# Second layer's weighing carried into the next head, and three short groups in the context preparation

## What is computed

```python
# prepared once from the context
K1, V1 = ctx @ Wk1 + bk1, ctx @ Wv1        # second layer, 16 heads of width 16
K3, V3 = ctx @ Wk3 + bk3, ctx @ Wv3        # last layer
V2     = ctx @ Wv2                         # third layer, 16 heads of width 64
# second layer's cross attention, for each head h of 16
s   = q[h] @ K1[h].T / 4 + fside[0, h]     # 128 x 12544, fside is an input of 103 MB
p   = exp(s - max(s));  att[h] = (p @ V1[h]) / sum(p)
# second layer's state space: a causal filter of length 128, the sum of 64 exponentials per channel
```

## Time and profile before

| what | value |
|---|---|
| median of 3 runs | 3325.09 us (3325.0 to 3327.77) |
| profiled execution, its own time | 3318.68 us |
| its span, first to last instruction | 3317.0 us |
| mean granted TensorE clock | 0.965 |
| busy: PE, DVE, ACT, POOL | 92%, 45%, 44%, 7% |
| context preparation | from the start to about 770 us |
| second layer's cross attention | about 1005 to 1517 us |
| third layer's cross attention | about 1600 to 2638 us |

### The profile page before, as it was taken

How to read it: one execution, slowest core, us unless ns; L and a number is a source line. 1 busy time by engine, 2 the same in 40 slices (tenths; PEclk the granted TensorE clock), 3 DMA queues, 4 the chain that set the end, 5 groups by cost and what they waited for, 6 DMA issues and landing times. The chain is left out here.

```text
span 3317.0 us, 66321 instructions
## 1 busy us (share of the span) xinstructions
PE 3054.6 (92%) x23699; PEld 1942.3 (59%) x23699; DVE 1481.3 (45%) x4098; ACT 1471.5 (44%) x2522; POOL 247.3 (7%) x178
## 2 busy tenths in 40 slices
PE   7999999998787999998899999999999887999979
PEld 5555555556484666664455555555555674666678
DVE  2223232321525777765333333333333326888632
ACT  2333333333313888883144444444444432656621
POOL 3231313130000000000000000000000002000000
PEclk9999999999897999999899999999999987999979
DMA  7878787877248999964311111111111254565355
GB/s 227 250 253 255 253 256 254 254 243 228 88 172 327 369 372 359 362 266 166 152 40 41 55 58 39 58 58 39 58 58 39 84 181 116 148 157 147 100 189 193
DMA packets 303301, 577.59 MB, mean 174 GB/s; under 512 B 79666, under 2 KB 249432, under 8 KB 291928
## 3 DMA queue, kind: packets, MB, share of 16 engines
q1 hardware_dynamic: 303204, 576.36, 51.4%
HBM read 395.34 MB, written 180.97 MB: 174 GB/s over the span
## 5 line engine op out<-in xcount | busy, mean ns | idle before, releaser
L1644 DVE TENSOR_SCALAR_CACHE_REDUCE all_S<-l2x_scores 128x448 f32<-128x448 f32 x448 | 261.1, 621 | 413.8 <-PE l2x_scores L1559 413.8
L1708 ACT COPY early_nat_in<-l2x_key_bank 128x448 f32<-128x448 f32 x224 | 119.2, 532 | 486.5 <-PE l2x_key_bank L1546 484.5
L1546 PE MATMUL l2x_key_bank<-ahead_ctx,early_nat_out 128*64 128x448 f32 x1536 | 331.0, 552 | 0.0
L500 PE MATMUL prep_work<-prep_wv,prep_ctxT 128*128 128x512 f32 x688 | 299.9, 594 | 0.0
L887 DVE CUSTOM_DVE_ANT_0 all_S<-l1x_scores,l1x_bias 128x448 f32<-128x448 f32 x448 | 261.9, 621 | 74.4 <-PE l1x_scores L799 67.4
L1138 DVE TENSOR_REDUCE l3x_rowmax<-l3x_scores 128x1 f32<-128x448 f32 x448 | 263.5, 623 | 39.6 <-PE l3x_scores L1058 38.1
L1220 ACT ACTIVATE l3x_pT<-l3x_turned 128x896 f32<-128x896 f32 x224 | 205.0, 918 | 170.3 <-PE l3x_turned L1066 167.1
L1582 PEld LDWEIGHTS l2x_out<-l2x_pT,l2x_v_half 128*64 128x64 f32 x3136 | 203.5, 137 | 96.8 <-issue 96.6
L954 ACT ACTIVATE all_S<-all_S,l1x_negmax 128x896 f32<-128x896 f32 x224 | 232.8, 1042 | 48.5 <-DVE l1x_negmax L900 33.1
L1723 ACT ACTIVATE all_S<-all_S,l2x_negmax 128x896 f32<-128x896 f32 x224 | 233.7, 1044 | 25.2 <-DVE l2x_total L1662 23.8
L1559 PE MATMUL l2x_scores<-early_nat_in,early_nat_out 64*128 64x448 f32 x896 | 229.1, 588 | 8.9 <-ACT early_nat_in L1708 8.2
(11 more groups left out here) (652 smaller groups left out, 4264.6 us busy)
## 6 DMA issues: line engine op xcount, KB each, us to landing
l1x_bias<-in_fside_Bx16xSxS_dram SPq DMA_DIRECT2D x112, 896.0 KB, 6.9
scratch_k<-prep_kparts SPq DMA_DIRECT2D x84, 672.0 KB, 3.3
l1x_k_half<-scratch_k SPq DMA_DIRECT2D x32, 1568.0 KB, 9.7
l2x_v_half<-scratch_v SPq DMA_DIRECT2D x32, 1568.0 KB, 6.3
l3x_k<-scratch_k SPq DMA_DIRECT2D x32, 1176.0 KB, 7.2
scratch_k<-prep_kparts SPq DMA_DIRECT2D x56, 448.0 KB, 4.8
scratch_v<-prep_st_v SPq DMA_DIRECT2D x12, 2048.0 KB, 9.1
scratch_v<-prep_st_v SPq DMA_DIRECT2D x12, 1536.0 KB, 7.2
```

Source lines behind the costliest of these rows:

```text
L500: last = nc.tensor.matmul(w[:, h, :], ctxT[:, k, j * P:(j + 1) * P], wv2[:, k, h * 512:(h + 1) * 512], start=(k == 0), stop=(k == KT - 1))
L1546: last = nc.tensor.matmul(keys_ps[half * VW:(half + 1) * VW, 0:HB], wk_cur[:, k, :], ahead.piece[c // 2][:, k, cols], start=(k == 0), stop ...
L1644: nc.vector.tensor_scalar(com.S[:, b * HB:(b + 1) * HB], scores_ps[half][:, 0:HB], 1.0, -3.4e38, ALU.mult, ALU.max, accum_out=rowmax[:, b: ...
```

## The change

**Second layer.** `head_stream` is split. The first layer keeps a plain version with one head, whose work is the same. The second gets `head_stream_biased`. TensorE's step c < 5 now also weighs block c + 9 of the head before, and the five weighings behind step 13 stand only behind the last head. The sum of the strips of head h - 1 stands in step 6 of head h. Two PSUM banks take the strips in turn (the second is the bank `last`), the sum goes into a free part of the same bank. VectorE copies the strips and takes the reciprocal in step 5, divides in step 7. TensorE's and VectorE's loops hold two heads. In the queue, the second value half of head h now stands behind bias block 1 of head h + 2, and the first value half of head h + 1 behind its bias block 5.

**Preparation.** `LATE = 3`, `KEPT = 3`: three short groups with three `v2` steps each. The filter's steps are 12 per group (`PER = 6`), the last group is written out behind the loop and takes the last 8. The late values are four blocks of each of three groups; those of the third group are read from context piece 1. Their stores have 4, 4, 2 and 2 blocks.

```diff
-LATE = 2
-N_LATE = LATE * (GC - 1)
+LATE, KEPT = 3, 3
+N_LATE = LATE * (GC - KEPT)
+STORES = ((0, KEPT, 4), (1, KEPT, 4), (2, KEPT, 2), (2, KEPT + 2, 2))
...
-    PER = 5
+    PER = 6
...
-        short, all_steps = plan[:10], plan
+        short, all_steps = plan[:9 + KEPT], plan
...
-        STEPS_AT = {"s": {10: range(0, 5), 12: range(5, 10)}, "v": {11: range(0, 5), 13: range(5, 10)}}
+        STEPS_AT = {"s": {10: range(0, 6), 12: range(6, 12)}, "v": {11: range(0, 6), 13: range(6, 12)}}
+        LAST_STEPS = states.total - (GRP - 1 - LATE) * states.n
...
-            with engine.Fori(LATE, GRP) as g:
+            with engine.Fori(LATE, GRP - 1) as g:
                 one(g, plan)
+            one(GRP - 1, plan)
...
-                    store(g, ((0, 1),))
+                    store(g, ((0, KEPT),))
...
-                states.rest(states.vector_step, dve, GRP - LATE)
...
-                states.rest(states.scalar_step, act, GRP - LATE)
...
+    banks = [ph.ps("out", [P, 512]), last_ps]
...
+        def load_head(h, first=False, second_of=None, first_of=None):
+
+            for i in range(GRP // 2):
+                load_bias(h, i, first)
                 if i == 2:
-                    load_keys(sp, k, 0, first)
+                    load_keys(h, 0, first)
                 if i == 6:
-                    load_keys(sp, k, 1, first)
-            if v is not None:
-                if i == 3:
-                    load_values(sp, v, 0, first)
-                if i == 6:
-                    load_values(sp, v, 1, first)
+                    load_keys(h, 1, first)
+                if i == 1 and second_of is not None:
+                    load_values(second_of, 1, first)
+                if i == 5 and first_of is not None:
+                    load_values(first_of, 0, first)
...
+        load_head(0, first=True, first_of=0)
+        load_values(0, 1, True)
+        load_head(1)
+        load_head(2, first_of=1)
+        with sp.Fori(1, HEADS - 2) as h:
+            load_head(h + 2, second_of=h, first_of=h + 1)
...
-    def tensor_head(pe, h, following):
-        for c in range(GRP + lag):
-            if c < GRP:
-                turn(pe, h, c)
-                if following:
-                    scores(pe, h + 1, c)
+    def tensor_head(pe, h, odd, first=False, following=True):
+        for c in range(GRP):
+            turn(pe, h, c)
+            if following:
+                scores(pe, h + 1, c)
             if c >= lag:
-                weigh(pe, h, c - lag)
-        if tiles > 1:
-            sum_tiles(pe, h)
...
+                weigh(pe, h, odd, c - lag)
+            elif not first:
+                weigh(pe, h - 1, 1 - odd, c - lag + GRP)
+            if c == lag + 1 and not first:
+                sum_tiles(pe, h - 1, 1 - odd)
...
+        with pe.Fori(0, HEADS // 2 - 1) as i:
+            tensor_head(pe, i * 2 + 1, 1)
+            tensor_head(pe, i * 2 + 2, 0)
...
+    def leave_bank(dve, h, odd):
+        dve.wait_ge(weighed, h * GRP + GRP + ring)
+        nc.vector.tensor_copy(out_parts[:, :], banks[odd][:, 0:P]).then_inc(parts_ready, 1)
         dve.wait_ge(rowsum_taken, h + 2)
         nc.vector.reciprocal(inverse[:, :], total[:, :]).then_inc(out_step, 1)
+
+    def divide(dve, h, odd):
         dve.wait_ge(out_step, h + 1)
...
+    def vector_head(dve, h, odd, first=False, following=True):
         for c in range(GRP):
             if by[c] == "v":
                 copy_turned(dve, nc.vector.tensor_copy, h, c)
             if following:
                 take_scores(dve, h + 1, c)
+            if c == lag and not first:
+                leave_bank(dve, h - 1, 1 - odd)
+            if c == lag + 2 and not first:
+                divide(dve, h - 1, 1 - odd)
         if following:
             max_of(dve, h + 1)
-        leave(dve, h)
+        sum_of(dve, h)
...
-        pieces = [(i, c, half) for i in range(LATE) for c in range(1, GC) for half in range(2)]
+        pieces = [(i, c, half) for i in range(LATE) for c in range(KEPT, GC) for half in range(2)]
...
+                    if n == 2 * 2 * (GC - KEPT):
+                        pe.wait_ge(ahead.loaded[1], 16)
-                    at = (i * GC + c) * P
+                    at = (i % 2 * GC + c) * P
```

More of the change, by code:

```diff
@@ new lines, in turn, with weigh @@
+    def turn(pe, c):
+        pe.wait_ge(exp_done, c + 1)
+        if c >= 2:
+            pe.wait_ge(copied[by[c - 2]], rank[c - 2])
+        for i in range(GC):
+            last = nc.tensor.transpose(turned_ps[c % 2][:, i * P:(i + 1) * P],
+                                       com.S[:, (c * GC + i) * P:(c * GC + i + 1) * P], com.ident[:, :])
+        last.then_inc(turned, 1)
+    def weigh(pe, c):
+        pe.wait_ge(v_loaded[c], 16)
+        pe.wait_ge(copied[by[c]], rank[c])
+        for i in range(GC):
+            k = c * GC + i
+            last = nc.tensor.matmul(out_ps[:, 0:vw], pT[c % ring][:, i * P:(i + 1) * P],
+                                    v_half[k // (CH // 2)][:, k % (CH // 2), :], start=(k == 0), stop=(k == CH - 1))
+        last.then_inc(weighed, 1)
@@ new lines, in on_scalar @@
+    def on_scalar(act):
+        act.wait_ge(negmax_ready, 1)
+        for c in range(GRP + 2):
+            if c < GRP:
+                s = com.S[:, c * GW:(c + 1) * GW]
+                nc.scalar.activation(s, s, ACT.Exp, bias=negmax[:, 0:1], scale=1.0,
+                                     accum_out=rowsum[:, c:c + 1]).then_inc(exp_done, 1)
+            if c >= 2 and by[c - 2] == "s":
+                copy_turned(act, nc.scalar.copy, c - 2)
+    run.on_sync, run.on_tensor, run.on_vector, run.on_scalar = on_sync, on_tensor, on_vector, on_scalar
@@ L744, in load_bias @@
             sp.dma_start(bias_tile[i][:, :], bias(h, i)).then_inc(bias_loaded[i], 16)
-    def load_values(sp, h, j, first):
-        if not first:
-            hold(sp, held, weighed, (h - 1) * GRP + GRP // 2 * (j + 1) + ring)
-        if heads == 1:
-            for at in range(GRP // 2):
-                c = j * (GRP // 2) + at
-                sp.dma_start(v_half[j][:, at * GC:(at + 1) * GC, :], v_src(h, c)).then_inc(v_loaded[c], 16)
-            return
-        sp.dma_start(v_half[j][:, :, :], v_src(h, j)).then_inc(v_loaded[j], 16)
@@ L757, in load_head, with load_values @@
-    def load_head(sp, k, v, first=False):
-        for i in range(GRP // 2):
-            if k is not None:
-                load_bias(sp, k, i, first)
+        def load_values(h, j, first):
+            if not first:
+                hold(sp, held, weighed, (h - 1) * GRP + GRP // 2 * (j + 1) + ring)
+            sp.dma_start(v_half[j][:, :, :], v_src(h, j)).then_inc(v_loaded[j], 16)
+        def load_head(h, first=False, second_of=None, first_of=None):
+            for i in range(GRP // 2):
+                load_bias(h, i, first)
@@ L855, in on_tensor @@
-    def on_tensor(pe, before_scores=lambda pe, h: None):
-        if tiles > 1:
-            pe.wait_ge(cleared, 1)
-        if more_scores:
-            before_scores(pe, 0)
-            for c in range(GRP):
-                if ctx_loaded is not None and c % 2 == 0:
-                    pe.wait_ge(ctx_loaded[c // 2], 16)
-                scores(pe, 0, c)
-        if heads > 1:
-            with pe.Fori(0, heads - 1) as h:
-                before_scores(pe, h + 1)
-                tensor_head(pe, h, True)
-        tensor_head(pe, heads - 1, False)
+        nc.tensor.matmul(banks[odd][:, P:P + VW], out_parts[:, :], select[:, :], start=True, stop=True).then_inc(summed, 1)
@@ L959, in on_scalar @@
     def on_scalar(act):
-        if heads > 1:
-            turn = 4
-            with act.Fori(0, heads // turn) as g:
-                for j in range(turn):
-                    scalar_head(act, g * turn + j)
-        else:
-            scalar_head(act, 0)
+        turn = 4
+        with act.Fori(0, HEADS // turn) as g:
+            for j in range(turn):
+                scalar_head(act, g * turn + j)
     run.on_sync, run.on_tensor, run.on_vector, run.on_scalar = on_sync, on_tensor, on_vector, on_scalar
```

274 lines of the change are left out of this document (145 added, 129 removed).

## The result

| what | before | after |
|---|---|---|
| median | 3325.81 us (3325.0 to 3329.86, 5 runs) | 3346.82 us (3345.18 to 3347.6, 5 runs) |
| profiled execution, its own time | 3318.68 us | 3347.23 us |
| its span | 3317.0 us | 3345.5 us |
| mean granted TensorE clock | 0.965 | 0.960 |

The ratio is 1.0061, with a 95% interval of 1.0047 to 1.0074: the changed kernel is slower, by 21 us. The two profiled executions lie 28.5 us apart, since that of before is 7 us under its kernel's median, while that of after lies at its kernel's median.

What follows compares the result with a forecast made beforehand. TensorE was taken to bound preparation and the heads' steps that turn, score and weigh. Preparation -12, late values 0, heads +20 and clock +14 gave +22 us on the median of 3325.09: 3347 us, range 3316 to 3364.

Steps and rivals of the forecast that it cites:

- Preparation: Context preparation: three short groups of 41.3 us and fewer stalls make it 11.6 us shorter, bounds 5 and 14.
- the stalls' end: Context preparation: ScalarE's value copy comes due 6.8 us later and finds its stores done; 2 us of stalls left.
- the queue's room: Preparation's second group: with 1.05 MB more the queue needs 288 GB/s of 311, so the key stores fit.
- State steps and late values: Preparation's state steps moved into the groups, and late values with their four stores: each worth 0.
- Heads at full clock: Second layer's heads: period 29.77 us, 1.24 more; 20 us slower in all, bounds 13 and 24.
- The boundary's gain: Second layer, turn 13 to the next turn 0: 4.49 us for 5.25, a gain of 0.76 us.
- The charge of 0.1 a head: Second layer's heads: cost of the sum's products in step 6 and VectorE's copy and reciprocal, 1.4 us in all.
- The clock: TensorE idles 2.2 us at head boundaries and its clock falls: 8.5 falls of 1.7 us, 14 us slower.
- The order of the values: SyncE's value loads moved between bias blocks in the second layer's heads: worth 0.
- The clock holds: Rival, second layer's heads: the idle time costs no clock; +8 us, 3333 us; chance 0.23.
- The weighings cost only themselves: Rival, steps 0 to 4 of a head: moved weighings cost 0.43 us each and fill waits; 3318 us; chance 0.17.
- Preparation doesn't do what it says: Rival, context preparation: key stores set the pace, +7 us for -12, 3366 us; chance 0.08.

Runs made afterwards that it cites:

- e1: Kernel before with only the change's edits of the preparation and the late values, heads as before: 3310.7 us, ratio 0.9965.
- e9: e5 with the wide values of a short group stored block by block, three stores with 256-byte rows for one with 768-byte rows: 3316.6 us, ratio 0.9968.
- e11: e5 with ten state steps a group for twelve, so that 18 stand behind the last group: 3309.4 us, ratio 0.9946.
- e2: Kernel before with only the change's edits of the second layer's heads (head_stream), preparation as before: 3391.9 us, ratio 1.0207.
- e7: e2 with 30 filler products on TensorE at each head boundary: 3380.7 us, ratio 1.016.
- e8: e2 with the preparation's last context group written out behind its loop, the same work: 3370.5 us, ratio 1.0135.
- e3: Changed kernel with 30 products of no use to the result behind step 13, filling most of TensorE's idle time at each boundary: 3330.7 us, ratio 1.002.
- e6: e5 with SyncE's value halves in the order of the kernel before: 3311.1 us, ratio 0.995.
- e12: e3 with SyncE's value halves in the order of the kernel before: 3334.5 us, ratio 1.0025.
- e5: Changed kernel with the five weighings put back behind step 13, only the sum carried into the next head: 3311.0 us, ratio 0.9951.
- e4: Changed kernel with 10 filler products behind step 13, leaving part of TensorE's idle time at each boundary: 3337.0 us, ratio 1.0043.
- e10: e5 with ScalarE looping over eight heads instead of four: 3308.4 us, ratio 0.9946.

## Why the prediction was right, and where it was not

The median came out at 3346.8 us for 3347 forecast. The mechanism was the one forecast: the period of a head, turn 0 behind the exponential, the lower clock behind the idle time and the shorter preparation all show in the trace. That the number is right to less than a microsecond is luck. Terms of 3 and 6 us erred in opposite directions, and a difference under some 7 us can't be told from none with this kernel.

**Preparation, -12 forecast, -12.2 in the trace, -12 to -14 in e1.** The size of a group (41.3 forecast, 41.4 to 41.5 measured) was right. The reason given for the stalls' end covers one of the two. A copy that waited for a value store comes due later in a longer group, and that wait is gone even in e9, which keeps the length. But the stall at 129.57 us stood behind a key store, and for these I had only the queue's room. There the form of the store counts: with rows of 256 bytes, e9 has key waits of 4.7 and 5.3 us and loses 8.5 of the 12 us. This is what the Trainium skill (DMA: Bandwidth & Descriptors, the table of properties) says with its 512 bytes for full rate, and I had weighed it at 2 us. In direction the measurement agrees with it: 512 KB in short rows took 9.9 us to land, 1536 KB in longer ones 13.1.

**State steps and late values, 0 forecast.** e11 shows it for the steps, even with 18 of them behind the last group. For the late values there is no run of their own; e1 contains them, and the preparation's 12 us account for its whole gain. The stage that makes them took 51.5 to 53.6 us in the four traces with the old stores (before, e2, e7, e8) and 50.9 to 54.0 in the ten with the new ones.

**Heads at full clock, +20 forecast, +16.6 measured** (e3: 449.3 for 432.7). The boundary's gain was 0.78 us (4.47 for 5.25) for 0.76, turns 0 to 5 took 9.64 for 9.65, and the period was 29.69 for 29.77. Three small terms failed. The charge of 0.1 a head for the sum and VectorE's copy was nothing: step 6 takes 2.09 us, step 7 then 2.01, together what 1.84 and 2.25 were. Turns 5 to 13 became 0.04 us shorter. And head 0, whose boundary gains as the others do while its own first steps hold no weighing, was left out: it takes 29.5 us in the changed kernel and 29.9 in e3, for 30.6.

**The clock, +14 forecast, +20 measured.** This is the term that was mis-sized. I took half of the ordinary boundaries to lose the clock, since 2.2 us lay between an idle time that lost it (2.31) and one that kept it (2.01), and 1.7 us a fall. In heads 1 to 14 the trace has 13 falls of 14: the three with a table load, and ten of the eleven ordinary ones, at 1.4 to 1.57 us each. The two errors, 3.4 us too much for the heads and 6 too little for the clock, partly cancel; the forecast's own total for heads and clock was 34, and it was 36.3, with 1.0 more in head 15, which I had put at 0.

**The order of the values, 0 forecast:** e6 and e12 show it, in both arrangements.

**The rivals.** "The clock holds" was given 0.23 and 3333 us; e3 makes it hold and takes 3331. "The weighings cost only themselves" fell: with the clock held, steps 0 to 4 still took 9.64 us, 1.85 for a step with a weighing, as in the rest of the head. Its price of 0.43 us belongs to weighings that run one behind the other (e5: six in 2.58 us). "Preparation doesn't do what it says" fell by e1: the waits for key stores shrank from 10.3 to 3.6 us there too. Its place was well chosen, though, as e9 shows.

**What I did not see.** The heads' part alone is 67 us slower, not 34, because VectorE stalls in its loop of two heads when the code before it is that of the old preparation. The change escapes this; in e8 writing the last context group out is enough for it. A side of the change that I had put at nothing (the group written out) is therefore worth 21 to 24 us to the other part (e8 for e2: 3370 for 3392 us, 1.0135 for 1.0207; 26.8 us in the heads of the two traces), and no row of before could show it: there VectorE looped over one head.

## What to carry to other kernels

Work at the end of an iteration that fills a wait is cheap. Moved into a stretch where its engine is the bound, it costs its full price there, and it leaves a hole that can cost the clock as well. Before emptying such a hole, ask what will be in it; here the products that did nothing (e3) bought 14 to 18 us, and the better cut was to move only the part that makes others wait, the sum, and leave the weighings where they filled the wait (e5: ratio 0.9951 for 1.002 of e3, 20 us in the spans and 23 by the ratios). And when a loop body grows, look for "issue" idle times at its turn-back and at the instruction queues' packets, in the kernel as it is finally put together: a part tested alone can stall where the whole does not.

## What the runs showed of the hardware

- TensorE's idle times of 1.48 and 1.64 us kept the clock in all heads of e4 and e3; of those of 2.07 to 2.15 us ahead of heads 1 to 15, 11 of 12 lost it in the changed kernel, while in e2 and e8 single ones of 2.14 and 2.15 us kept it; those of 2.76 us (e4) and 3.42 us (the changed kernel), at table loads, lost it each time. A fall in the changed kernel cost 1.4 to 1.57 us, spread over some 3.3 us of work at the lower level; single ones in e2, e4 and e8 cost 2.7 to 2.9. In another place of the kernel before 2.01 us had kept it.
- VectorE, with a body of two heads, stood still up to 6.3 us at the loop's turn-back and up to 3.7 us soon after, 52 to 53 us in all (36.3 + 15.8 in e2, 35.6 + 17.3 in e7); with the same body behind other code it did not (e8, and the changed kernel). ScalarE, with eight heads in its loop, stood still for 3.66 us (e10).
- ScalarE's table load of 1.28 us comes once per pass of its loop, and not with each head: looping over eight took two of three away.
- Packets of 256 bytes took 21 ns on average and packets of 768 bytes 45 ns in the preparation (e9 and e5, 19 to 160 us).
- Over single heads the queues moved 371 to 375 GB/s (e5, and the earlier trace rows), and over heads 1 to 13 together 364 (before) and 367 (e5).
